# Turning k and the normalized attention result by DMA instead of TensorE in a fused retention and FP4 linear kernel

## What is computed

```python
xn  = layernorm(x)
q, k, v = heads((xn @ Wq + bq) * hd**-0.5), heads(xn @ Wk + bk), heads(xn @ Wv + bv)   # 16 heads of 64
ret = (q @ k.T) * D                     # D[i, j] = exp(decay_h * (i - j)) for i >= j, else 0
ret = ret / clip(abs(ret.sum(-1)), 1, None)
g   = (ret @ v), normalized over each head's 64 features, * gn_w + gn_b
attn = (silu(xn @ Wg + bg) * g) @ Wo + bo
ffn  = quantize_nvfp4(xn) @ quantize_nvfp4(weight).T * output_scale + bias
out  = x + attn + ffn
```

## Time and profile before

| | us |
|---|---|
| median of 3 runs | 2128.29 (2125.03 to 2128.88) |
| the profiled execution | 2123.72 |
| its span, first to last instruction | 2121.9 |
| TensorE busy | 2052.4 (97% of the span) |
| VectorE busy | 1628.9 (77%) |
| GpSimd busy | 728.7 (34%) |
| ScalarE busy | 661.3 (31%) |

### The profile page before, as it was taken

How to read it: one execution, slowest core, us unless ns; L and a number is a source line. 1 busy time by engine, 2 the same in 40 slices (tenths; PEclk the granted TensorE clock), 3 DMA queues, 4 the chain that set the end, 5 groups by cost and what they waited for, 6 DMA issues and landing times.

```text
span 2121.9 us, 53476 instructions
## 1 busy us (share of the span) xinstructions
PE 2052.4 (97%) x19218; PEld 1154.4 (54%) x19218; DVE 1628.9 (77%) x4375; ACT 661.3 (31%) x1318; POOL 728.7 (34%) x512
## 2 busy tenths in 40 slices
PE   5989899999999999999999999999999999999999
PEld 2544455555555555555555555555555555555544
DVE  8899888988899897667777667776767877766732
ACT  5755632332232322223232222222222323222300
POOL 1223233432343343244333234333234333334320
PEclk9999999999999999999999999999999999999999
DMA  8988734334434333323423323323333333233343
GB/s 311 295 271 266 237 97 127 109 109 128 104 126 138 126 92 102 107 89 124 115 85 113 94 89 125 120 83 114 89 100 114 124 95 103 95 95 108 124 155 118
DMA packets 181864, 276.69 MB, mean 130 GB/s; under 512 B 117376, under 2 KB 117504, under 8 KB 181504
## 3 DMA queue, kind: packets, MB, share of 16 engines
q1 hardware_dynamic: 181776, 275.53, 40.5%
HBM read 205.23 MB, written 41.42 MB: 116 GB/s over the span
## 4 chain that ended last, share of the span: by engine, by line
PE 66%; DVE 27%; issue 4%; DMA 2%; ACT 1%; SPq 0%; DVEq 0%; ACTq 0%
PE mm L1352 31%; PE mm L1369 10%; PE mm L1284 6%; PE tp L1284 6%; PE mm L1293 4%; DVE xa L898 2%; PE four L1424 2%; DVE state L1103 2%; DVE xa L897 2%; PE four L1437 1%; DVE xa L903 1%; PE four L1293 1%; DVE xa L902 1%; DVE qs L878 1%; DVE gst L1117 1%
## 5 line engine op out<-in xcount | busy, mean ns | idle before, releaser
L1352 PE MATMUL mm<-xnT,wring 128*128 128x512 f16 x4800 | 1072.5, 381 | 18.5 <-ACT kT L717 8.1
L1352 PEld LDWEIGHTS mm<-xnT,wring 128*128 128x128 f16 x4800 | 463.6, 98 | 556.4 <-issue 18.8
L594 POOL TENSOR_TENSOR yT<-gn,gate 128x512 f32 (+1 forms) x64 | 83.8, 1310 | 806.1 <-ACT gn L770 806.1
L759 ACT ACTIVATE work<-four,gs 128x64 f32<-128x64 f32 x512 | 158.1, 414 | 592.1 <-DVE gs L1130 592.1
L1369 PE MATMUL mm<-wring,xnT 128*128 128x256 f16 x2688 | 302.6, 273 | 0.0
L1369 PEld LDWEIGHTS mm<-wring,xnT 128*128 128x128 f16 x2688 | 262.8, 98 | 36.3 <-DVE res L1233 0.2
L1284 PE MATMUL mm<-wo,yT 128*128 128x512 f16 x960 | 214.1, 380 | 0.4
L577 POOL TENSOR_TENSOR qparts<-qT,qparts 128x512 f16<-128x512 f32 x64 | 77.9, 1217 | 343.8 <-ACT qT L717 343.8
L1117 DVE BATCH_NORM_STATS2 gst<-four 128x6 f32<-128x64 f32 x512 | 73.5, 216 | 144.7 <-PE four L1437 143.9
L1284 PEld LDWEIGHTS mm<-wo,yT 128*128 (+1 forms) x960 | 90.9, 98 | 108.3 <-issue 0.8
L577 POOL TENSOR_TENSOR kparts<-kT,kparts 128x512 f16<-128x512 f32 x64 | 83.7, 1308 | 131.7 <-ACT kT L717 131.7
(11 more groups left out here) (202 smaller groups left out, 2811.7 us busy)
## 6 DMA issues: line engine op xcount, KB each, us to landing
wring<-parts SPq DMA_DIRECT2D x252, 512.0 KB, 4.3
xt<-in_x SPq DMA_DIRECT2D x34, 512.0 KB, 3.6
out<-res SPq DMA_DIRECT2D x32, 512.0 KB, 3.0
parts<-wo SPq DMA_DIRECT2D x28, 512.0 KB, 6.0
res<-in_x SPq DMA_DIRECT2D x28, 512.0 KB, 3.6
ftile<-in_w_f SPq DMA_DIRECT2D x12, 512.0 KB, 5.8
parts<-wring SPq DMA_DIRECT2D x8, 512.0 KB, 6.5
probs<-in_x SPq DMA_DIRECT2D x5, 512.0 KB, 4.6
```

What stands on the lines that cost most here:

```text
L594: nc.gpsimd.tensor_tensor(hi, gn[:], gate[:, u], ALU.mult)
L759: last = nc.scalar.activation(work[:, c * P + h * HD:c * P + (h + 1) * HD], ao[h][:, c * VW:c * VW + HD], ACT.Identity, bias=gs[:, 1, g:g ...
L1352: last = MM(mm[n % 2][:], wring[:, slot, wj, k, :], xnT[:, parity, xj, k, :], start=(j == 0), stop=(j == 3 * KT - 1))
```

## The change

From group two on, the four turning steps leave TensorE. SyncE issues DMA transposes of 16-bit data in their place, and because an f32 value can't be turned so, its f16 high and low parts are turned and added again.

For k (`move_k`, `join_k`, `scale_k`): the two parts in `kparts` exist already for the scores. When the low part is written, one DMA transpose [128 x 1024] moves both, turned, over `kT`; GpSimd adds them into `kn`; ScalarE scales `kn` in place. For the normalized result (`n_hi`, `split_n`, `move_n`, `join_n`, `affine_n`): ScalarE writes the high part of `work`, GpSimd the low part, two DMA transposes [128 x 512] move them into `yT`, GpSimd adds them into `gn`, ScalarE applies gn_w and gn_b in place, and `gate_y` goes on as before. The low part of the next body's first k is now written at the end of a body (`split_next_k`), between `split_n(1)` and `join_n(1)`. `qs`, `ones` and `f_row` moved into other tiles to make room for `nparts`; the last `MIDDLE` body is written out alone so that the reload for `TAIL` comes earlier.

```diff
+                def move_k(u):
+                    w("kq_split", 2 * u + 1)
+                    sp.sem_inc(sp_turn, 1)
+                    sp.dma_start(k_turned.rearrange("p a (c x) -> p (a c) x", x=P),
+                                 kparts[:].rearrange("p a t -> p (a t)"), transpose=True).then_inc(s["k_moved"], 16)
+                def move_n(u):
+                    w("n_split", n_use(phase, u))
+                    for j in range(2):
+                        sp.dma_start(yT[:, parity, j, ds(q * 2 + u, 1), :].rearrange("p a (c t) -> p (a c) t", t=P),
+                                     nparts[:, j], transpose=True).then_inc(s["n_moved"], 16)
...
                 load_slice(0, 0)
+                move_k(0)
                 load_slice(0, 2)
                 load_gates()
                 move_x_parts()
                 w("xq_ready", 1)
                 load_x(1)
                 load_slice(1, 0)
+                move_k(1)
                 load_v(0)
                 load_slice(1, 2)
                 load_v(1)
+                if last:
+                    reload_late()
+                move_n(0)
                 w("out_ready", 1)
                 sp.dma_start(a["out"][rows, :], res[:]).then_inc(s["out_stored"], 16)
                 move_x()
+                move_n(1)
...
+                def split_n(u):
+                    w("nhi_ready", n_use(phase, u))
+                    nc.gpsimd.tensor_tensor(nparts[:, 1], work[:], nparts[:, 0], ALU.subtract).then_inc(s["n_split"], 1)
+                def join_n(u):
+                    w("n_moved", 2 * n_use(phase, u))
+                    pool.sem_inc(pool_turn, 1)
+                    hi, lo = (yT[:, parity, j, ds(q * 2 + u, 1), :].rearrange("p a t -> p (a t)") for j in range(2))
+                    nc.gpsimd.tensor_tensor(gn[:], hi, lo, ALU.add).then_inc(s["n_joined"], 1)
+                def join_k(u):
+                    w("t0_full", u)
+                    w("k_moved", u + 1)
+                    nc.gpsimd.tensor_tensor(kn[:].rearrange("p c h d -> p (c h d)"), k_turned[:, 0], k_turned[:, 1],
+                                            ALU.add).then_inc(s["k_joined"], 1)
...
                 evacuate(0, 0)
                 evacuate_v(0)
-                affine(1, 1)
                 x_hi()
                 evacuate(0, 2)
-                decay_k(0)
+                affine_n(1, 1)
                 evacuate_v(1)
+                scale_k(0)
                 evacuate(1, 0)
                 evacuate(0, 3)
-                decay_k(1)
+                scale_k(1)
                 evacuate(1, 2)
                 normalize(0)
+                n_hi(0)
                 evacuate(1, 3)
-                affine(0)
+                affine_n(0)
                 normalize(1)
+                n_hi(1)
```

More of the change, by code:

```diff
@@ L136, in mm_use, with n_use, run_phase @@
     return 2 * u + 1 + n // 2
-def run_phase(eng, phase, body):
+def n_use(phase, u):
+    return 0 if phase == FIRST else u + 1
+def run_phase(eng, phase, body, last_body=None):
     if phase == MIDDLE:
         for g in range(GROUPS - 3):
-            with eng.Fori(0, CH) as q:
+            alone = last_body and g == GROUPS - 4
+            with eng.Fori(0, CH - 1 if alone else CH) as q:
                 body(MIDDLE, q + g * CH, (g + 3) % 2, q, g + 3)
+            if alone:
+                last_body(MIDDLE, CH - 1 + g * CH, (g + 3) % 2, CH - 1, g + 3)
     elif phase == FIRST:
@@ L540, in _ @@
                     sp.wait_ge(xq1_kept, 16)
[L541 to L547, removed]
+                run_phase(sp, phase, body, lambda *at_body: body(*at_body, last=True))
             for name in ("out_stored", "w_k", "w_v", "w_q", "w_g"):
@@ L569, in _, with body @@
             nc.gpsimd.tensor_tensor(out_bias[:], out_bias[:], res[:], ALU.add).then_inc(bias_sum, 1)
-            def body(phase, i, parity, q, group):
+            def body(phase, i, parity, q, group, last=False):
                 w = waiter(pool, phase, i)
@@ L638, in body @@
                     add_biases()
+                split_n(0)
+                join_n(0)
                 gate_y(0)
+                split_n(1)
+                if not last:
+                    split_next_k()
+                join_n(1)
                 gate_y(1)
@@ L644, in _ @@
                     pool.wait_ge(v_bias_in, 16)
-                run_phase(pool, phase, body)
+                run_phase(pool, phase, body, lambda *at_body: body(*at_body, last=True))
         @block.scalar
@@ L752, in copy_v, with scale_k, n_hi, affine_n @@
                                          ACT.Copy).then_inc(s[f"t{bk}_free"], 1)
+                def scale_k(u):
+                    w("k_joined", u + 1)
+                    for h in range(2):
+                        last = nc.scalar.activation(kn[:, :, h, :], kn[:, :, h, :], ACT.Copy,
+                                                    scale=kfac[:, ds(q * 4 + 2 * u + h, 1)])
+                    last.then_inc(s["kn_ready"], 1)
+                def n_hi(u):
+                    w("normed", u + 1)
+                    nc.scalar.activation(nparts[:, 0], work[:], ACT.Copy).then_inc(s["nhi_ready"], 1)
+                def affine_n(u, back=0):
+                    w("n_joined", n_use(phase, u - 2 * back))
+                    at_pair = ds(q * 2 + 1 + u - 2 * back, 1)
+                    nc.scalar.activation(gn[:], gn[:], ACT.Identity, bias=gnp[:, 1, at_pair],
+                                         scale=gnp[:, 0, at_pair]).then_inc(s["gn_ready"], 1)
                 def normalize(u):
@@ L1255, in sum_slices @@
                 at_batch = slice(SLICES * b + first, SLICES * b + first + count)
-                MM(slice_sums[:, first:first + count], ones[:], maxs[:, at_batch], start=True, stop=True)\
+                MM(slice_sums[:, first:first + count], ones, maxs[:, at_batch], start=True, stop=True)\
                     .then_inc(summed, 1)
@@ L1450, in body @@
                     project_v(0)
-                if phase != FIRST or i:
+                if phase == FIRST and i:
                     transpose_g(1, 1)
```

112 lines of the change are left out of this document (81 added, 31 removed), and 4 rows, old and new, of the table PER.

## The result

The changed kernel takes 2258.09 us (median of 4 runs, 2257.51 to 2260.88) against 2128.59 for the kernel before beside it (2125.03 to 2129.06): a ratio of 1.0615, 95% interval 1.0596 to 1.0633. It is 6.2% slower; 2205 us and 3.6% were forecast. The direction and the place were right, the size was too small by 53 us.

A forecast was written before the change was run, and what follows sets the result against it. TensorE was taken to bound the middle, TensorE and VectorE together groups two and three. 2123.7 + 52 (groups two and three) + 24 (middle) = 2200 us profiled, plus 4.6 for the median: 2205 us, 3.6% slower, range 2100 to 2290.

The forecast's parts named there:

- My forecast: Whole kernel: the case the prediction held likeliest, 2150 to 2250 us, chance 0.64.
- What bounds the kernel: Middle groups bound by TensorE (63.30 of 63.30 us busy); groups two and three by TensorE and VectorE together.
- What leaves TensorE, 1.9 us a body: Four turning steps leave TensorE in each of 28 bodies: about 1.9 us a body, 53 us.
- The price of GpSimd on VectorE, 0.7 us per us: VectorE loses 0.7 us for each us of GpSimd work beside it.
- Groups two and three, 6.5 us a body, 52 in all: Eight bodies there each lose 5.3 us on VectorE plus 1.2 us of new waits: 52 us.
- The middle, gating at T+18.1, GpSimd's run to T+34.8: In a middle body starting at T, gating waits for `affine_n(1, 1)` until T+18.1; GpSimd is then busy until T+34.8.
- k lands 3.3 us after its issue: Pair 1's k transpose in a middle body, issued at T+39.6, lands 3.3 us later, at T+42.9.
- `scores(1)` waits 3.1 us: In each middle body TensorE reaches `scores(1)` at T+44.7 and waits 3.1 us for q's split, done at T+47.8.
- The middle body, 64.5 us: Each of 20 middle bodies goes from 63.3 to 64.5 us, +1.2, together +24 us.
- VectorE's busy time: Sign for the whole kernel: the prediction is wrong if VectorE's busy time hardly grows.
- Transposes land late: Rival: in middle bodies pair 1's k transpose lands later than 3.3 us; 2260 us at 6 us, 2355 at 10.8; chance 0.10.
- The cover holds: Rival: VectorE loses under 2 us a body and `scores(1)` doesn't wait; faster, 2075 to 2090 us; chance 0.20.

The follow-up runs named there:

- e8: Kernel before with only k turned by DMA, in the middle groups alone, q's split and evacuation ahead of k's join and scaling: 2111.11 us, ratio 0.9930.
- e10: Groups two and three as in the kernel before; in the middle the whole change with the orders of e5: 2105.31 us, ratio 0.9907.
- e5: Kernel of e2, with ScalarE's `affine_n(1, 1)` also moved ahead of evacuating q of pair 0: 2147.55 us, ratio 1.0097.
- e3: Kernel before with six more GpSimd instructions a body from group two on, no DMA transposes added: 2168.68 us, ratio 1.0204.
- e6: Changed kernel with only the half on the normalized result; k turned by TensorE as before: 2163.20 us, ratio 1.0175.
- e2: Changed kernel with pair 1's q split and decayed ahead of k's join, and evacuated ahead of k's scaling: 2175.93 us, ratio 1.0235.
- e1: Changed kernel with pair 1's k transpose issued ahead of the wait for the quantized x and the loads behind it: 2188.98 us, ratio 1.0295.
- e9: Kernel before with six more DMA transposes a body from group two on, into a tile nobody reads: 2129.29 us, ratio 1.0015.
- e4: Kernel before with only the k half of the change; the normalized result turned by TensorE as before: 2149.15 us, ratio 1.0111.

## Why the prediction was right and where it fell short

The direction, the range and the two places of the loss were right, and the wait that was forecast for the middle is there. The time lies 53 us above the forecast, and also above the 2150 to 2250 that it gave under "My forecast". In the profiled executions the span grew by 134.6 us, where 52 + 24 = 76 were forecast: 59 too little, of which 9 lie in groups two and three, 48 in the nineteen middle bodies (70.8 measured, 19 x 1.2 = 22.8 forecast) and 2 in the rest.

- **What bounds the kernel**, and that groups two and three lose while the middle loses through a late `scores(1)`: right. e8 and e10 win only by leaving the former alone and freeing the latter.
- **What leaves TensorE, 1.9 us a body**: 1.6. With all waits gone a middle body is 61.7 us (e5), not 61.4.
- **The price of GpSimd on VectorE, 0.7 us per us**: e3 measured 0.44 on the time of groups two and three; I had read it off quantization halves, the instructions that suffer most. Here the estimate was too high.
- **Groups two and three, 6.5 us a body, 52 in all**: 7.6, 60.8 in all, within the bounds. By e3, 3.6 of them are the six instructions; that leaves 4.0 for new waits and for the clock (12 stretches at half clock lie there as well, before one), where I had put 1.2. That the sum came out nearly right is luck, for its parts were wrong both ways: that the normalized result is a link of the ring there, and costs 5.7 a body by itself with its four additions (e6), was not seen.
- **The middle, gating at T+18.1, GpSimd's run to T+34.8**: 18.4 and 34.8. `xq_ready` at T+38.3: 37.2. k's transpose issued at T+39.6: 38.5.
- **k lands 3.3 us after its issue**: 5.3. This is a mis-sized term: 52 of the 64 transposes in rows 9 had no load of 512 KB under way when they were issued, and this one comes right behind two (last section). The trace of before had the better number: its other 12 landed after 4.9 us in the median. The read for the join came at T+43.7 (forecast T+42.9, since the issue was 1.1 us earlier), q's split at T+48.4 (T+47.8).
- **`scores(1)` waits 3.1 us**: 2.62 in this body (2.8 on average), since TensorE came there 1.12 us late already. That earlier wait, for the carry behind the slowed second half, is the step that I left out: I had followed VectorE to `xq_ready` but not to the states behind it.
- **The middle body, 64.5 us**: 65.4 where nothing else disturbs it (61.7 + 1.12 + 2.62), so 0.9 above the forecast. That is 17 of the 48 us. Another 8 are the first middle body (73.3 instead of 65.4), which the forecast took for one like the others. The mean of 66.7 of the other eighteen is 1.3 us above 65.4, which makes the remaining 23. Some 16 of them are TensorE's clock (ten stretches that cost 1.6 us each, an estimate from the two times of the 24 matmuls in the last section), for which the sum had no term.
- **VectorE's busy time** was to grow, or the prediction to be wrong. It fell by 53 us, and the mechanism held all the same. *The transposes land later than 5 us* was another sign of a wrong prediction, and it came true as well (5.3). By its own tests the prediction failed on two of three; the third, the wait at the scores, is the one that tells of the mechanism. The tests were badly chosen. So was "over 1.2 us on average" for the quantization instructions: no line of them has a mean over 1.12 us, since in the change the first half ran at nearly full speed in the middle. And *VectorE busy nearly throughout* in groups two and three was wrong: 56.18 of 68.70 us in the body shown, a smaller share than before, with bodies of 69.8 us on average where 66 to 69 were forecast.
- **The rivals.** *Transposes land late*: half right, each was 2 us later than forecast, behind the loads that this rival named, but the earlier issue took back half of it, and e2 shows that the landing is harmless once q doesn't stand behind it. *The cover holds*: no, yet e10 shows that this rival needed only two orders and the middle alone.

## What to carry to other kernels

When work leaves the bound engine for others, follow each value on its new way through every in-order queue, and put nothing that TensorE needs soon behind the part that waits for a DMA: two swaps of neighbouring steps were worth 82 us here, more than the 45 us (28 x 1.6) that left TensorE. Work added to GpSimd must be placed beside VectorE instructions that have slack, and VectorE's busy time doesn't tell whether it was; the waits behind VectorE do. Where stages differ, decide stage by stage: the change costs 61 us where VectorE is full and, with the orders of e10, gains 24 (over nineteen bodies) where it isn't. And a DMA transpose on a chain that counts belongs ahead of the large loads: behind one it took 2 us longer to land here.

## What was unexpected of the hardware

**The clock after short waits.** Windows of a middle body of the changed kernel, columns as above, the granted clock third from the end:

```profile
1404.00:1407.00 3.00, 0.50 (x3) 0.00 (x0) 0.73 (x5) 3.00 (x9) 1.10 (x1) 1.00 0.45 147
1408.00:1411.00 3.00, 3.00 (x8) 1.05 (x8) 0.71 (x2) 1.48 (x3) 1.67 (x2) 0.50 0.02 5
1412.00:1415.00 3.00, 3.00 (x26) 1.28 (x28) 0.00 (x0) 0.00 (x0) 0.69 (x1) 1.00 0.24 47
```

```profile
1407.20 0.57 PE L1514 MATMUL four<-qparts,kparts 64*64 64x64 f16 x48 [2.70 <-POOL qparts L619]
1407.90 6.98 PE L1406 MATMUL mm<-wo,yT 128*128 128x512 f16 x24
```

TensorE had been idle 2.70 us for q; then the clock stood at half, 1.2 instead of 2.4 GHz, and the 24 matmuls behind took 6.98 us instead of 5.35. Over the whole span there are 27 such stretches in the changed kernel, 113 us together, and 5 in the kernel before, 24 us. e10_middle_only has 6 and 31 us. Twelve of the 27 lie in the middle, where the kernel before has none. Eleven of them begin 0.3 to 1.5 us after one of the 20 waits at `scores(1)` (2.3 to 3.4 us of idle TensorE), the twelfth at the wait of 4.2 us in the first middle body. None follows one of the 20 waits for the carry, of 1.1 to 1.7 us. Not every long wait is followed by one: nine of the 20 are not, and behind the 2.62 us in the body above the matmuls took 5.35. What decides between the eleven and the nine is open. That the waits cause the stretches is borne out by e1 and e2: both take away the waits at `scores(1)` and leave all transposes and additions in, and one stretch is left in the middle. e9, with 5 in all, shows that the DMA transposes alone make none.

**The landing of k's transpose.** It takes 5.3 us (4.7 to 6.8) from `kparts` to `kT`, for the same 128 x 1024 values that take 3.3 us in `move_x_parts`. e1 moved pair 1's transpose, and no other, ahead of the loads of 512 KB:

```profile
1671.03 1.24 SPq L403 DMA_TRANSPOSE kT<-kparts  x1
...
DMA to landing us min/median/max: 3.1/4.4/7.1
```

The median of 4.4 is a mixture: pair 1's land after 3.2 us (3.1 to 4.0) there and pair 0's, right behind a load as before, after 5.2 (4.7 to 7.1). e4 and e8 agree: pair 0's is issued there with no load under way and lands after 3.1 us, pair 1's right behind the loads after 5.2 and 5.3. Of e9's spare transposes the first of each body, right behind the load of x, lands after 4.5 us in the median, and the second, issued when the first has landed, after 3.1. `move_x_parts` in the kernel before divides the same way: 52 transposes issued with no load under way landed after 3.3 us in the median, 12 with one after 4.9. So the 2 us go with a load under way when the transpose is issued. How the transpose and the load hold each other up no run shows.
